# A wait for the landing of each group's gathers, on GpSimd, in the first two edge passes of a four-layer graph kernel

## The reference

```python
h = relu(layernorm(x)); x = x + L0(h)    # gated graph layer: edge sum, then a GRU cell per node
h = relu(layernorm(x)); x = x + L1(h)    # graph convolution: edge sum, W, layernorm
h = relu(layernorm(x)); x = x + L2(h)    # relational layer, sums by source
h = relu(layernorm(x)); x = x + L3(h)    # attention by softmax over the incoming edges
# L0:  messages = segment_sum(h[src] @ W_msg.T + b_msg + edge_embed[type9], dst)
#      h_new = gru_cell(messages, h)
# L1:  agg = segment_sum(norm * h[src], dst)   (with a loop at each node)
#      out = layernorm(agg @ W.T + b) * gamma + beta
```

## Time and profile before

| | us |
|---|---|
| three timed runs | 10877.73, 10886.74, 10894.94 |
| median | 10886.74 |
| the profiled execution, span | 10879.4 |
| first pass, first gather to last (L721) | 133.0 to 2490.4 |
| second pass, first gather to last (L988) | 2537.8 to 4920.8 |

### The profile page before, as it was taken

The page is one execution under the profiler, slowest core; times in us unless marked ns, Lnnn a source line. Parts: engine busy times, 40 slices in busy tenths (PEclk is TensorE's granted clock), DMA queues, the critical chain, the costliest instruction groups (busy, mean ns, idle before and its releaser), DMA issues. The chain is left out here.

```text
span 10879.4 us, 143542 instructions
## 1 busy us (share of the span) xinstructions
PE 7281.4 (67%) x34582; PEld 5619.6 (52%) x34582; DVE 4894.6 (45%) x12591; ACT 1925.5 (18%) x5149; POOL 6900.4 (63%) x6291
## 2 busy tenths in 40 slices
PE   2555555554666666668888888888836666666667
PEld 2444444443333333336777777777724555555555
DVE  5444444444665565654222222222264555555556
ACT  1111111111111111112222222222221111111111
POOL 3666666665666666665888888888815555555553
PEclk6555555555555555556777777777755555555555
DMA  6222222222222222223444444444472222222222
GB/s 236 56 56 58 57 56 58 55 57 59 74 71 74 75 71 76 71 75 66 56 56 55 56 56 56 55 56 56 53 212 67 68 68 65 67 66 67 65 66 52
DMA packets 809417, 765.69 MB, mean 70 GB/s; under 512 B 128472, under 2 KB 701362, under 8 KB 809073
## 3 DMA queue, kind: packets, MB, share of 16 engines
q0 software_dynamic: 375872, 414.65, 22.5%
q1 hardware_dynamic: 340391, 271.94, 8.2%
q10 hardware_dynamic: 92938, 77.03, 2.3%
HBM read 544.72 MB, written 224.78 MB: 71 GB/s over the span
## 5 line engine op out<-in xcount | busy, mean ns | idle before, releaser
L1412 POOL DMA_INDIRECT scat<-msg_out,msg_idx x1564 | 2414.3, 1544 | 491.5 <-issue 319.8
L2001 POOL DMA_INDIRECT soft_rows<-proj,soft_slot x1564 | 1487.5, 951 | 1385.1 <-DVE soft_x L2188 718.2
L721 POOL DMA_INDIRECT L_rows<-H,L_slot x1568 | 1493.2, 952 | 993.3 <-issue 596.3
L988 POOL DMA_INDIRECT L_rows<-H,L_slot x1568 | 1496.5, 954 | 890.4 <-issue 464.5
L1505 PE MATMUL msg_ps_msg<-msg_hb,msg_lhs 128*128 128x128 f32 x6272 | 1600.9, 436 | 1.2 <-DVE msg_lhs L1478 1.2
L1505 PEld LDWEIGHTS msg_ps_msg<-msg_hb,msg_lhs 128*128 128x128 f32 x6272 | 1493.0, 328 | 185.3 <-issue 183.9
L1478 DVE SCALAR_TENSOR_TENSOR msg_lhs<-msg_dst_sp,msg_node,msg_ps_c 128x512 f32<-128x512 f32 x784 | 551.2, 745 | 2040.4 <-ACT msg_dst_sp L1433 1813.0
L2130 PE MATMUL soft_ps_sum<-soft_onehot,soft_x 128*128 128x64 f32 x3136 | 752.8, 422 | 306.0 <-DVE sums_b L2247 216.9
L861 PE MATMUL L_sum<-L_onehot,L_rows 128*128 128x64 f32 x3136 | 691.0, 392 | 392.9 <-issue 337.6
L2130 PEld LDWEIGHTS soft_ps_sum<-soft_onehot,soft_x 128*128 128x128 f32 x3136 | 705.6, 328 | 371.3 <-issue 276.8
L861 PEld LDWEIGHTS L_sum<-L_onehot,L_rows 128*128 128x128 f32 x3136 | 657.9, 305 | 433.9 <-issue 423.6
(11 more groups left out here) (365 smaller groups left out, 10133.3 us busy)
## 6 DMA issues: line engine op xcount, KB each, us to landing
L_rows<-H,L_slot POOLq DMA_INDIRECT x3136
msg_hb<-HB SPq DMA_DIRECT2D x392, 128.0 KB
soft_at_in<-in_edge_attr_dram SPq DMA_DIRECT2D x195, 256.0 KB
scat<-L_zeros SPq DMA_DIRECT2D x64, 408.0 KB
rel_parts<-scat SPq DMA_DIRECT2D x100, 256.0 KB, 5.2
HB<-L_prod ACTq DMA_DIRECT2D x49, 512.0 KB
scat<-msg_out,msg_idx POOLq DMA_INDIRECT x1564
soft_rows<-proj,soft_slot POOLq DMA_INDIRECT x1564
```

Of the source, the lines that this page charges most:

```text
L721: pool.indirect_dma_start(rows[:, k, j, :], None, t["H0"], bass.IndirectOffsetOnAxis(ap=slot[:, k, j:j + 1], axis=0)).then_inc(gathered[k] ...
L988: pool.indirect_dma_start(rows[:, k, j, :], None, t["H1"], bass.IndirectOffsetOnAxis(ap=slot[:, k, j:j + 1], axis=0)).then_inc(gathered[k] ...
L1412: pool.indirect_dma_start(t["scat"][j], bass.IndirectOffsetOnAxis(ap=idx[:, k, j:j + 1], axis=0), out[:, k, j, :], None, compute_op=ALU.ad ...
L2001: pool.indirect_dma_start(rows[:, s % SC, j, :], None, t["proj"], bass.IndirectOffsetOnAxis(ap=slot[:, s, j:j + 1], axis=0)).then_inc(gath ...
```

## The change

After the four gathers of a group POOL waits until `gathered[k]` has reached the count that this group brings it to (r is the turn of the loop, and J is 4), in both passes; an empty instruction holds the wait. The later phases are as before. No instruction is moved, and nothing is changed on PE, ACT, DVE or SP. The last group of the first pass, which is padding, issues its gathers or is left out as before, and its wait with it.

```diff
@@ first edge pass, gather() on GpSimd
                     pool.indirect_dma_start(rows[:, k, j, :], None, t["H0"],
                                             bass.IndirectOffsetOnAxis(ap=slot[:, k, j:j + 1], axis=0)
                                             ).then_inc(gathered[k], 16)
+                pool.wait_ge(gathered[k], r * (16 * J) + 16 * J)
+                pool.nop(nofuse=True)
             with_nodes(pool, S, t, [(0, gather)], [])
```

## The result

The changed kernel takes 11,864 us (median; 11,842 to 11,870) against 10,882 us before, a ratio of 1.0901 [1.0886, 1.0917]. It is slower, as forecast, and within the range, but 294 us above the 11,570 that I named. The profiled execution has a span of 11,839.9 us, 960.5 more than before.

What follows compares the result with a forecast made beforehand. POOL's own gather issuing nearly bound the kernel, with pauses when the ring of eight groups ran dry. Adding 356 and 342 us for the passes, less 12, to 10,879.4 gave 11,565, named as 11,570 us; range 11,400 to 11,870.

Steps and rivals of the forecast that it cites:

- The mechanism: In both passes, gathers stay 0.947 us, 2.2 us idle precedes every group, index-copy waits nearly vanish, "remote" falls.
- the landing: From the fourth gather's end to its count reaching POOL: 1.42 us a group, ends 1.25 and 1.6.
- The price of a group: Time of a whole group with the wait, 4.69 + 1.42 + 0.77 + 0.05 = 6.93 us, against 6.02 and 6.055 before.
- the restart: From the wait's release to POOL's next gather: 0.77 us, ends 0.30 and 0.9; plus 0.05 for `idx_ready` and branch.
- The ends of the passes: With PE close behind POOL at each pass's end, about 6 us saved twice: -12 us.
- The ends of the terms: Low landing gives 6.71 us a group, 11,400 us; high landing, restart and rest give 7.29 us, about 11,850 us.
- late counts stay late: PE's counts still miss POOL's stop, the ring runs dry every third group: +300 us, 11,870 us; chance 0.18.
- the prepared restart: Next gather is prepared under the wait, only 0.30 us follows the landing: 6.41 us a group, 11,165 us; chance 0.09.
- the cheap gather: Gathers get cheaper on an empty queue; at 0.65 us each the kernel takes about 10,640 us; chance 0.01.
- the wait holds: Denies the rival that POOL's count is already met and nothing changes: 10,887 us, chance 0.02.
- The figure beside the sum: The skill page's 2.15 us from a gather's issue to completion: 6.72 us a group, about 11,410 us.
- the meaning of the pauses before: POOL's 3.0 us pauses every 2.9 groups read as PE's counts arriving late while POOL issues, not shown cause.

Runs made afterwards that it cites:

- the second set: Change in first pass alone, two waits a group, one fill, two fills, each against the kernel before at 9,322 us: 1.0999, 1.3676, 1.0341, 1.1059.
- the third: Set of the kernel before (11,012 us), the changed kernel, a wait for three of four gathers, and a wait every fourth group: 1.0002, 1.0838, 0.9912, 1.0054.

## Why the prediction was right, and where its sum was short

**The mechanism** held in every point that could be checked in rows. A gather inside a group stays at 0.947 us in the median with 0.30 between; the gap stands before every group alike; the waits for the index copy vanish; "remote" vanishes. PE and the others keep the pace, waiting for the gathers. The wait one group back (gap 0.30, ratio 1.000) and the second wait in a group (+1.97 us) show that the landing is what is paid, once per wait that holds.

**The price of a group was mis-sized**: 6.93 us forecast, 7.352 measured. The 0.42 us are made of
- the landing, 1.65 in the mean for 1.42 (+0.23). Not half of it is typical: the median is 1.52. The rest is that I took a typical value and no tail. Of the gaps before a group about a tenth (82 of 782) are above 2.8 us, as that at 2424.33 in the timeline, and they make up some two thirds of the 0.14 by which the mean gap, 2.56, lies above the median, 2.42.
- the restart, 0.91 in the mean for 0.77 + 0.05 (+0.09). The 0.77 was right: 0.76 us is what the kernel with two waits has where nothing stands behind the landing. What I had put too low is the 0.05 for the rest: with the met wait for `idx_ready` it is 0.12 us more at each group, with the branch 0.24 more once in eight, 0.15 together.
- the three gaps inside a group, 0.325 in the mean for 0.30 (+0.07), and the four gathers, 0.955 for 0.947 (+0.03). Here too I had used the rows' medians.

In the second pass it is the same: 7.365 for 6.93. Over both passes these terms are 165 + 159 = +324 us. The ends of the passes gave 32 us, not 12. PE, waiting for each group, is close behind when the last gather lands: its last product of a group starts 4.2 and 4.4 us after the last gather. In the kernel before it is 11.0 us in the first pass, from which I took the 6 for both, but 27.2 in the second (4920.8 to 4948.0). And a later phase took 26 us less. Those offset 49 us, and the miss is 324 - 49 = 275 us on the span of 11,565 forecast.

**The ends of the terms** did their work. The upper ones (landing 1.6, restart 0.9) lie close to the measured means (1.65, 0.91), and the range's 11,870 holds the result with 6 us to spare, narrowly.

**The rival "late counts stay late"** had forecast 11,870, nearly the measured time, and it is wrong. It needed pauses of over 3 us at every third group, ACT standing as long behind "remote", and neither is in the rows. By the time alone one would have picked it. That it was near is chance: 0.38 us a group for pauses that never came against 0.42 us for terms cut too short. The other rivals are out by the same rows: no gap near 1.7 us (the prepared restart), no gather under 0.938 us in any run (the cheap gather), and the wait holds.

**The figure beside the sum.** The Trainium skill ("DMA: Bandwidth & Descriptors", section "Anatomy of one DMA — SWDGE (gpsimd) path") had 2.15 us from issue to completion for 64 KB. The traces have 2.4 us at the least and 2.5 in the median to the landing (the last row shown for the change in the first pass alone). By the page's figure the kernel would have come out at 11,410, 450 us short; the measurement decides.

**What the prediction had right only by half** is the meaning of the pauses before. It read them as PE's counts reaching the others late while POOL issues without a break, and said that this was not shown. That the counts come late is so: in the kernel before, about half of the first pass's index copies that wait for a product (193 of 384) start over 0.5 us after its end, up to 19 us, though ACT stands idle. But POOL's issuing alone isn't the cause, since in the second set it issues through a whole pass and no count comes late. The runs bear out the half that decides: a stop of 2.5 us at each group ends both the late counts and the pauses. But the sum did not say what this is worth. Where the pauses are absent, a pass of the kernel before takes 5.045 us a group, and the change would cost (7.37 - 5.045) x 782 = +1,820 us (an estimate, ratio about 1.195; one pass of it was measured at 1.0999). Where they are present, 1.0 us a group of the wait is paid with the time of the pauses, and 1.09 is left. So about 45% of the wait's price never showed.

## What to carry to other kernels

A wait for a DMA's landing on the engine that issues the DMAs costs the whole landing plus the restart at each wait that holds (2.55 us here), and nothing when it aims at something already landed: put it as many transfers back as the dependence allows. Price it by the mean and not by a typical row, since the tail of the landings counts 391 times. And when a wait appears to cost less than its length, look for the pause that it has replaced: that pause may be absent the next time, as it was in one of the three sets here.

## What the runs showed of the hardware that I had not expected

- **The late counts are not always there.** In the second set the kernel before took 9,322 us, 14 to 15% less than elsewhere. A pass without the change runs at 5.045 us a group there instead of 6.0 to 6.2 (one was traced), and a later phase with gathers (`soft_rows`) takes 1,975 us there, not 2,669 as in the trace of before, with POOL's 718 us of waits for DVE's `soft_x` gone. If both passes run so, together (0.975 + 1.04) x 391 + 694 = 1,482 of the 1,560 us between the levels. The phase of scatters between them takes 2,888 to 2,890 us in either. The second set and the third bear the same chip number, 6, and lie at different levels, so if that number names one chip, the chip is not what decides. What does was not tested.
- **Short stops end POOL's pauses, but it takes long ones to bring the counts through.** For each index copy of the first pass that waits for a product, the traces give the time from the product's end to the copy's start. Summed where ACT stands idle before it, this lateness is 1,750 to 1,850 us in the two traces of the kernel before and in those with a wait at every fourth or eighth group; 1,580 us with stops of 1.2 us at every group (none over 12.6 us); 351 with stops of some 2.5 us at every second (none over 3.7); and 48 with 2.56 us at every group, as in the kernels of the second set (47). The wait for three gathers and the wait at every second group make POOL stand about as long in all (1.0 and 1.1 us a group above the 0.30), so for the lateness the length of the single stop counts. Why it is so I can't say; no record shows where a count is in between.
- **The kernel with a wait for three gathers** is 0.9% faster than the kernel before where the pauses exist. Where they don't, it should lose by its 6.06 us against 5.045, some 800 us (an estimate, not run). It is therefore no version to adopt without knowing at which level the kernel will run.
- **The restart belongs to a gather behind a wait that held.** It is 0.76 us there, and 0.88 with one met wait behind the other. Behind a fill on POOL's own engine the gather follows after 0.28 us, as POOL's timeline in the kernel with two fills shows (the row is both fills together):

```profile
2003.41 1.18 POOL L730 MEMSET L_spare<- 128x512 f32 x2
2004.87 0.95 POOL L724 DMA_INDIRECT L_rows<-H,L_slot  x1 [0.28 <-issue]
```
